# Softmax attention: a spread order of TensorE's step, and PSUM banks shared out 4 and 3 between maxima and scores

## The reference

```
q, k, v = layernorm(x) @ Wq.T, @ Wk.T, @ Wv.T     # 16 heads of 16
q, k    = rope(q), rope(k)
attn    = softmax(q k^T / 4)                      # per head, 512 x 512
x       = x + (attn v) @ Wo.T
```

## Time and profile before

| | |
|---|---|
| median of three runs | 2517.26 us |
| the profiled execution, its own time | 2525.09 us |
| its span | 2523.4 us |
| granted TensorE clock, mean over the span | 0.966 |
| busy share of the span: TensorE, VectorE, ScalarE | 89%, 67%, 52% |
| `attention_mix` on the chip | about 231 to 1085 us |

### The profile page before, as it was taken

How to read it: one execution, slowest core, us unless ns; L and a number is a source line. 1 busy time by engine, 2 the same in 40 slices (tenths; PEclk the granted TensorE clock), 3 DMA queues, 4 the chain that set the end, 5 groups by cost and what they waited for, 6 DMA issues and landing times. The chain is left out here.

```text
span 2523.4 us, 48221 instructions
## 1 busy us (share of the span) xinstructions
PE 2240.6 (89%) x14822; PEld 1235.7 (49%) x14822; DVE 1699.2 (67%) x4310; ACT 1324.0 (52%) x2741; POOL 1138.2 (45%) x1495
## 2 busy tenths in 40 slices
PE   8997788888888888879989996999999969997987
PEld 5663122222222222256556664566666646655765
DVE  6777988888888888457653333777777748763322
ACT  5665676767776776645323333555555425432322
POOL 7985111111111111134326775777777724325776
PEclk9998799999999999989989998999999989998999
DMA  6664322222222221146857884011111026675886
GB/s 192 220 195 138 77 52 72 55 71 55 71 55 68 58 68 43 42 133 205 298 174 206 221 202 72 19 39 39 35 39 34 19 71 214 225 269 161 228 213 110
DMA packets 256150, 300.00 MB, mean 119 GB/s; under 512 B 24353, under 2 KB 241649, under 8 KB 255985
## 3 DMA queue, kind: packets, MB, share of 16 engines
q1 hardware_dynamic: 222208, 249.03, 32.3%
q0 software_dynamic: 29184, 46.43, 9.1%
q10 hardware_dynamic: 4592, 2.47, 0.4%
HBM read 192.13 MB, written 105.19 MB: 118 GB/s over the span
## 5 line engine op out<-in xcount | busy, mean ns | idle before, releaser
L708 DVE TENSOR_REDUCE a_row_max<-a_ps_m 128x1 f32<-128x512 f32 x1024 | 636.9, 683 | 38.3 <-PE a_ps_m L612 34.6
L768 ACT ACTIVATE a_probs<-a_ps_s 128x512 f32<-128x512 f32 x1024 | 528.7, 604 | 238.9 <-PE a_ps_s L638 237.6
L653 PE MATMUL a_ps_o<-a_probs,a_va 128*32 128x512 f32 x2048 | 275.1, 610 | 0.2 <-ACT a_o_sb L777 0.2
L1748 POOL TENSOR_TENSOR b_spread<-b_decay,held_own_sb 128x512 f32<-128x512 f32 x256 | 267.7, 1077 | 8.6 <-DVE b_weight L1809 8.6
L1809 DVE TENSOR_TENSOR b_weight<-b_ps_s,b_spread 128x512 f32<-128x512 f32 x256 | 163.8, 682 | 9.4 <-PE b_ps_s L1950 9.4
L612 PE MATMUL a_ps_m<-first_ks,first_qs 48*128 48x512 f16 x512 | 107.0, 415 | 69.4 <-DVE a_row_max L708 69.4
L612 PE MATMUL a_ps_m<-second 48*128 48x512 f16 x512 | 100.0, 387 | 55.0 <-DVE a_row_max L708 54.8
L551 POOL CAST a_high<-a_row_max 128x32 f16<-128x32 f32 x32 | 6.5, 204 | 307.3 <-DVE a_row_max L708 307.3
L590 POOL DMA_DIRECT2D x<-a_xo x32 | 24.2, 755 | 263.3 <-DVE a_row_max L708 223.5
L612 PEld LDWEIGHTS a_ps_m<-first_ks,first_qs 48*128 48x128 f16 x512 | 24.9, 94 | 207.9 <-DVE a_row_max L708 202.6
L1558 DVE SCALAR_TENSOR_TENSOR m2e_h<-m2e_act_g,m2e_xg,m2e_ps_h 128x192 f32<-128x192 f32 x64 | 26.5, 414 | 146.1 <-ACT m2e_act_g L1487 123.1
(11 more groups left out here) (397 smaller groups left out, 5331.7 us busy)
## 6 DMA issues: line engine op xcount, KB each, us to landing
parts<-second SPq DMA_DIRECT2D x16, 1536.0 KB, 6.2
rows<-m_early SPq DMA_DIRECT2D x32, 640.0 KB
m_early<-x SPq DMA_DIRECT2D x31, 512.0 KB
second<-parts SPq DMA_DIRECT2D x192, 64.0 KB
m_own<-in_L_ffn_w_gate_dram SPq DMA_DIRECT2D x24, 384.0 KB, 6.6
m_own<-in_L_ffn_w_up_dram SPq DMA_DIRECT2D x24, 384.0 KB, 7.1
m_early<-in_L_ffn_w_gate_dram SPq DMA_DIRECT2D x24, 384.0 KB, 4.8
m_early<-in_L_ffn_w_up_dram SPq DMA_DIRECT2D x24, 384.0 KB, 5.3
```

The costliest lines, as they stand in the source:

```text
L653: last = nc.tensor.matmul(ps_o[VW * j:VW * (j + 1), :], va[n.u][:, t, (h0 + j) * VW:(h0 + j + 1) * VW], probs[:, group % 2, j, t, :], star ...
L708: nc.vector.tensor_reduce(row_max[:, n.k // 4 % 2, t, e, n.p % 4:n.p % 4 + 1], m_bank(name, step)[:], AX.X, ALU.max).then_inc(m_drained, 1)
L768: nc.scalar.activation(probs[:, group % 2, j, t, :], s_bank(name, step)[:], ACT.Exp, scale=DK ** -0.5).then_inc(s_drained, 1)
L1748: nc.gpsimd.tensor_tensor(spread[:, n % 2, heads].rearrange("p h t c -> p (h t) c"), decay[:, n % 3, heads].rearrange("p h (t o) -> p (h t ...
```

## The change

Both ring sizes change, and so does the order of TensorE's stages. Before, a step ran quarter 0 of the maxima, quarters 0 and 1 of the scores, quarter 1 of the maxima, then one mix; and the same again for quarters 2 and 3, with `turn_att` ahead of the last mix. After it, each quarter of the maxima is followed by the same quarter of the scores, `mix_values(1)` stands behind scores 0 and `mix_values(0)` behind scores 2. No instruction is added or removed.

```diff
-    M_RING, S_RING = 3, 4
+    M_RING, S_RING = 4, 3
...
-            walk_pairs(pe, [(0, max_products(0)), (L_S, scores(0)), (L_S, scores(1)), (0, max_products(1)),
-                            (L_TURN, turn_shift), (L_MIX + 1, mix_values(1)), (L_OTURN, turn_output),
-                            (0, max_products(2)), (L_S, scores(2)), (L_S, scores(3)), (0, max_products(3)),
-                            (L_ATT[0], turn_att(0)), (L_ATT[1], turn_att(1)), (L_MIX, mix_values(0)), (L_OUT[0], project(0)), (L_OUT[1], project(1))])
+            walk_pairs(pe, [(0, max_products(0)), (L_S, scores(0)), (L_MIX + 1, mix_values(1)), (0, max_products(1)), (L_S, scores(1)),
+                            (L_TURN, turn_shift), (L_OTURN, turn_output),
+                            (0, max_products(2)), (L_S, scores(2)), (L_MIX, mix_values(0)), (0, max_products(3)), (L_S, scores(3)),
+                            (L_ATT[0], turn_att(0)), (L_ATT[1], turn_att(1)), (L_OUT[0], project(0)), (L_OUT[1], project(1))])
```

## The result

The changed kernel takes **2530.07 us** (median of 20 runs, 2520.38 to 2539.04) against 2524.57 us for the one before (20 runs beside it, on a chip a little slower than that of the three runs shown first): ratio **1.0022**, interval 1.0012 to 1.0033. It is slightly slower. I had forecast 2500, faster, with a range that ended at 2522.

A forecast was written before the change was run, and what follows sets the result against it. VectorE was taken to be paced by the maxima's ring of banks. Fifteen sequences gave -15.9 us and the ramp -3.3, together -19.2: 2498.1 from 2517.3, forecast as 2500, range 2474 to 2522.

The forecast's parts named there:

- The chains of waits: Eight steps of a sequence laid out from measured intervals: 49.56 us, 1.06 under 50.62, so -15.9 us over fifteen sequences.
- the maxima's ring: Mid-stage before the change: its loop takes 2.48 us for four reductions, where VectorE alone needs 2.40.
- the 1.08 us between pairs of scores: Score ring with three banks: two pairs of scores are at least 1.08 us apart.
- the 1.13 lost at r=1: Step r=1: scores 0 wait for the new shift, so VectorE's third reduction starts at 2.33 instead of 1.20 us.
- the waits ahead of the adds: Steps r=2 and r=4, with a projection: the residual add waits 0.94 and 0.61 us, in place of 1.7.
- too kind: Rival: the layout leaves out 0.06 us in each of eleven waits; no measurable change, 2508 us; chance 0.26.
- score ring: Rival: score ring becomes the bound, each of eleven waits grows by 0.25 us; slower, 2539 us; chance 0.12.
- the ramp: Stage start, maxima only: 36 reductions at 0.60 instead of 0.69 us each, 3.3 us less; bounds 0 and -5.
- the one on the clock: Fifteen sequences: clock was 1.00 despite TensorE's bank waits in each half step; no term for it in the sum.
- that rival: Rival: TensorE's clock falls, a tenth of the steps at half clock costs 25 us; 2525 and more; chance 0.02.
- the tail: Stage end, 1038 to 1086 us, no maxima: change taken as 0, between -2 and +3 us.
- the loop of 5.24 against 4.98: A plain step takes 5.24 us with the new order and rings, 0.26 longer than 4.98 before.

The follow-up runs named there:

- the two halves of the change: Kernel before with only the new ring sizes (2570.05 us, ratio 1.0243), and changed kernel's order with the old ring sizes (2516.23 us, ratio 1.0021).
- run 9: Not a run label: part of "makes the run 9 us slower than before", the 9 us corrected from 12 for 0.17 more in each wait.
- the filled kernel: Changed kernel with ten extra matmuls at r=1 in the shift wait, moved behind the bank wait; 2496.93 us, ratio 0.9954; again 2501.56 us, 0.9967.
- unfilled: Changed kernel with the shift wait at r=1 moved behind the bank wait, no matmuls added; 2518.87 us, ratio 0.9982; again 2507.42 us, 0.9990.
- by step: Changed kernel with lag 8's mix ahead of scores 0 at r=1 and lag 7's mix at the end of odd steps; 2507.15 us, ratio 0.9939.
- rings only: Kernel before with ring sizes 4 for maxima and 3 for scores, TensorE's order left; 2570.05 us, ratio 1.0243.
- by step, more: Kernel with order chosen by step, plus scores 3 ahead of maxima 3 in odd steps and extra matmuls in shift waits; 2508.56 us, ratio 1.0004.
- second pair of profiles: Profiles of the changed kernel and the kernel before, both run again on one chip; 2529.68 and 2524.25 us.
- The changed kernel again: Changed kernel run once more, nothing altered, on another chip; 2529.68 us, ratio 1.0026 to the kernel before.

## Why the prediction was wrong

**The chains of waits were right.** Every step of that part held: the maxima's ring as the pace of before, the 1.08 us between pairs of scores (1.06 and 1.07 measured), 49.56 us for eight steps (49.71), the 1.13 lost at r=1 (1.10), the waits ahead of the adds. The same way of laying out gave 54.1 and 50.2 to 50.8 for the two halves of the change before they ran, and 54.04 and 50.21 were measured. The rivals "too kind" and "score ring" are out for the changed kernel. (In the second one a sum is off: 0.17 more in each wait makes the run 9 us slower than before, not 12, with the 3.3 of the ramp taken off; nothing hangs on it.)

**The step that failed is the one on the clock.** I wrote that through the fifteen sequences the clock was 1.00 with TensorE waiting on banks, gave a fall 0.02, and had no term for it in the sum. Two things were wrong in it. The 1.00 in the earlier trace rows is a rounded mean, and hid a fall at 432.7 us, just where a shift wait had grown to 1.20 us. And I counted what the shift wait does to VectorE (1.13 us), not what it does to TensorE, which now stands still there for 1.2 to 1.3 us once a sequence. Each fall then costs 0.9 to 1.5 us for 3.4 us at half clock, as much as the sequence gains. The price that I gave that rival, half clock in a tenth of the steps and 25 us, was too high: between 300 and 1000 us the two profiles have 27 and 31 us at half clock, 4% of the time and 24 us more than the profiles of the kernel before, and the net cost is 8.5 and 7.9 us. That the time came near its 2525 is in part luck, since other terms missed in the same direction.

In the first pair of profiles the attention is 0.8 us longer, where the sum had 19.2 less. Of these 20 us the falls in the thirteen sequences are 8.5, the ramp 4.7, the last sequences and the tail 4.5, and 2.4 is gain that I had counted for fifteen sequences and that is seen in thirteen. That the clock decides is seen in the filled kernel: its attention is 14.1 us shorter than before, and its ratios of 0.9954 and 0.9967 make 2506 and 2509 us of the 2517.3, inside the range.

Filling the wait raises the clock and lowers the time (0.9954 and 0.9967 on two chips, against 1.0022 and 1.0026 for the changed kernel on others), and shortening it does so as well (0.9958, and 0.9982 for the swap of two waits). The filled and the changed kernel were not run on one chip. The pairs that were are changed and unfilled (1.0026 and 0.9982), and unfilled and filled (0.9990 and 0.9967, with intervals that just overlap). That the falls of the changed kernel come from TensorE's idleness at the shift wait of r=1 I take as shown.

Not shown is what makes a fall come at one of these waits and not at the next of the same length. In the two profiles of the changed kernel 13 of 24 waits of about 1.3 us at r=1 were followed by a fall; in those of the two unfilled runs 3 of 24 waits of about 1.2 us. Nor is a DMA needed, or a long wait: in the last kernel the falls follow a wait of 1.03 us for a bank, and by step had one behind pauses of under 0.5 us. The mean idleness is not it either: rings only has TensorE busy for 79% of 300 to 1000 us and no fall, the changed kernel for 87% and seven. The falls also often come 51.2 us apart, and a sequence with a fall takes nearly that long itself, so that the next wait meets the chip in the same situation; that is an observation, no test was made of it. The Trainium skill, "TensorE: Matmul & The Clock Gate", "HAM oscillation — how this bites in real kernels", has waits for DMA as what lets the clock fall in a matmul kernel. For the changed kernel the trace agrees with the kind of wait: its falls of mid-stage stand behind waits for the shift's DMAs, of 1.3 us and more. As the only kind it does not hold here: rings only waits for banks at every second pair of scores (0.7 us each) without a fall, but by step, more has its falls behind a wait of 1.03 us for a bank.

**The ramp was mis-sized.** The 36 reductions take 21.62 us, 3.3 less, as forecast:

```profile
230.04 21.62 DVE L708 TENSOR_REDUCE a_row_max<-a_ps_m 128x1 f32<-128x512 f32 x36 [5.08 <-PE a_ps_m L612]
```

But the steps behind them cost 4.7 more, outside my bound of 0. The second sequence has no outputs to turn or project yet, only plain steps, so it shows the loop of 5.24 against 4.98 with nothing won in return: 47.85 us from its shift copy to the next against 44.32. Eight times 0.26 are 2.1 of these 3.5 us; the rest is near the 1.1 that the shift wait at r=1 costs, 1.28 us there where the kernel before has none. I had the loss of 0.26 a plain step and that of r=1 in hand and did not apply them here. The second pair of profiles agrees, with 1.9 us more to the first residual add instead of 3.3 less.

**The tail** was +4.5 us instead of 0 in the first pair of profiles, outside its bound of 3, and +1.7 in the second, inside it. It holds the longest shift wait of all, and in the first pair 17.1 us at half clock behind it, against 6.8 before. In the second pair it is 6.8 against 3.4. The filled kernel has 3.4 there, and from the last shift copy to the next stage it takes 46.8 us (1023.69 to 1070.5), against 51.4 for the changed one (1033.77 to 1085.2) and 45.8 before. The changed kernel again takes 47.6 us there, and the unfilled one, with no time at half clock at all, 45.3. So what is missed there is again the clock, by a size that changes from run to run.

**Still open.** Profiles put the attention of the changed kernel at 0.8 us above and 2.1 us below that of the one before, while the medians say 5.5 us more (the two profiled executions lie 7.5 us above and 3.6 below theirs). The rest lies behind it, in stages whose instructions are the same, where single profiles differ by 13 and by 3 us. In the first pair these stages also have 28 us more at half clock (141 against 113), in the second as much as before (128). No experiment told chance from a cause.

## What to carry to other kernels

- With engines in order and rings of banks between them, write down each ring's loop (take up, process, free, and what stands between in the issue order) from the trace's own intervals, and add it up step by step. It gave the times of clean sequences within 0.4% where each wait was in it. The two misses were single waits left out: the bank that another use of the ring holds, and a copy in front of the instruction that frees the bank.
- A wait of TensorE is priced twice: for those who wait for its result, and for its clock. Where a reordering brings a wait of 1 us or more, for a DMA (1.3 us here) or for a bank (1.03), look for stretches at half clock behind it, and put later-needed work ahead of the waiting instruction (here one mix, 0.6% better than the change as it was).
- Read the granted clock in windows as short as the stalls. A mean of 1.00 over 759 us hid a fall.

## What I had not expected of the hardware

Ten matmuls more in each sequence, whose results are thrown away, made a kernel faster that is paced by waits: 2496.93 us at a granted clock of 0.968. A pause of TensorE of 1.3 us, among others of 0.2 to 0.6, was followed by a fall in about half of the sequences (13 of 24), one of 1.2 us in an eighth (3 of 24). And a stretch of 3.4 us at half clock costs a sequence of the changed kernel 0.9 to 1.5 us, not the 1.7 by which TensorE's own work grows; that VectorE's slack takes the rest is my reading, not tested.
